# Moving three pieces of work inside the turns of a pipelined attention layer

## The chip, the cores and the metric

One core of a Trainium2 chip runs the whole program. The metric is the device time of one execution in microseconds (us). TensorE, VectorE, ScalarE, GpSimd and SyncE (the profile's PE, DVE, ACT, POOL and SP) each run an instruction list of their own, in order, and meet only at semaphores.

## The reference

Two layers over 16 sequences of 256 tokens with 256 features. Each layer adds to the running rows `x` the output of a sequence mixer and of a mixture of experts, both computed from the layer-normalised rows. The first layer's mixer is a state-space scan, the second's is causal attention with 16 heads of 16 features. Only that layer is touched:

```python
xn = _layernorm(x)                       # per token, over 256 features
qkv = (xn @ w_qkv).reshape(b, t, 3, 16, 16)
scores = einsum('bqhd,bkhd->bhqk', q, k) * 0.25      # causal mask, then softmax
out = einsum('bhqk,bkhd->bqhd', softmax(scores), v).reshape(b, t, d) @ w_o
gate = softmax(xn @ gate_w.T)            # top 2 of 8 experts per token
x = x + out + experts(xn)
```

## The kernel before

X holds all rows of `x` on chip. The program runs in four stages: the first layer's normalisation, routing and shared expert; its expert tiles; its scan; then the second layer's attention, and its expert tiles. The change lies in the attention.

**The attention as a pipeline.** `static(NSEQ, 5, attention, first=1)` unrolls turns t = 1 to 19. Turn t works on five sequences at once: c = t, a = t - 1, b = t - 2, d = t - 3, o = t - 4, each present only while it lies in 0 to 15. Roughly:

- c: `combine` adds the first layer's expert outputs to X, `norm_stats` and `norm_apply` normalise (the power of the variance is GpSimd's).
- a: transposes of the normalised rows, router logits, queries and keys; the top-2 choice of experts (`pick_experts`, once for two sequences, when a is odd), ranks and places of the tokens (`rank_sums`, `place_slots`, when a is even).
- b: scores of its four groups of heads, and their row maxima.
- d: transposed scores, exponentials (ScalarE), masks (GpSimd), weighted sums (`weigh`), transposes of the mixed rows (`turn_mixed`), division by the sums (`normalise`).
- o: transposes (`turn_out`), output projection (`project_out`), sum into X (`add_out`).

Each engine has a function `attention` whose statements are that engine's order within a turn, written by hand. No planner moves anything.

**TensorE's order in a turn** (L2071 on). `scores(h, s, t)` is called eight times. It computes plain scores for half h of the four heads of group `s`, whose maxima VectorE takes, and transposed scores for `t`, whose maxima are already folded into the queries. Between the calls stand `turn_maxima(d, 1)`, `values`, `weigh(d, 0)`, then `turn_out`, `values`, then `weigh(d, 1)`, `norm_stage`, then `project_out(o)`, then `turn_maxima(b, 0)`, the ranking, the logits, `weigh(d, 2)`, then queries and keys, and so on. The sixth call is `scores(1, now(2), now(0))`; for its second part it waits for `qp`, which `shift(b, 0)` gives. The second call waits in the same way for `shift(d, 1)`. Ahead of `turn_maxima(b, 0)` stands a wait for `add_out(o)`, since both use the same bank of PSUM; ahead of `turn_maxima(d, 1)` one for the copy of the second keys, for the same reason.

**VectorE's order** (L1546 on). `maxima(r, i, h)` (L1519) are four masked reductions for group i. `shift(r, j)` (L1527) subtracts the transposed maxima from the queries. `normalise` (L1536, L1538) waits for `turn_mixed`. `norm_stats` is L1067, L1071 and L1074, `add_out` L1544, `norm_apply` L1087, and `pick_experts(1, i, [1])`, the choice of the second expert, L1127 to L1137.

**ScalarE** copies queries (L997) and keys (L1003) out of PSUM with head masks, `mixed_copy` is L992, the exponentials are L979. All matmuls are recorded under L1677, a helper; transposes stand under their own lines (`turn_maxima` L2061, `turn_mixed` L2068).

Of the kernel before, what the change touches and what calls it, by code (L numbers as in the profile page):

```python
# [19 lines left out]
NSEQ, SEQ, D = 16, 256, 256  # L20
# [116 lines left out]
def of(n):  # L137

    return Round(n // 2, n % 2) if 0 <= n < NSEQ else None
# [42 lines left out]
def is_first(r):  # L182

    return isinstance(r.n, int) and r.n < 2
# [8 lines left out]
def program(nc, ctx, a, out):  # L193
# [864 lines left out]
    def _(eng):  # L1058
# [106 lines left out]
        def place_tokens(l, m):  # L1165
            rank_sums(l, m)
            place_slots(l, m)
# [339 lines left out]
        def stats_stage(r):  # L1507
            A["comb"].wait(eng, r.n)
            norm_stats(1, r)
# [12 lines left out]
        def shift(r, j):  # L1522

            A["m"].wait(eng, 2 * r.n + j)
            for e in range(2):
                q = QM[r.u][:, e, j, :]
                ins = stt(q, bank[5][:, 0:SEQ], head_mask[:, 1 - e:2 - e], q, ALU.mult, ALU.add)  # L1527
            A["qp"].mark(ins)
# [12 lines left out]
        def add_out(r):  # L1541
            A["wo"].wait(eng, r.n)
            xs = X[:, bass.ds(r.n * CH, CH), :].rearrange("p c d -> p (c d)")
            A["add"].mark(tt(xs, xs, bank[5], ALU.add))  # L1544

        def attention(c, a, b, d, o):  # L1546
            if b:
                maxima(b, 0, 0)
            if d:
                shift(d, 1)  # L1550
            if b:
                maxima(b, 0, 1)
            if c and c.n > 1:
                combine(c, [0])
            if b and not a:
                place_tokens(1, NSEQ // 2 - 1)
            if b:
                maxima(b, 1, 0)
            if c and c.n > 1:
                combine(c, [1])  # L1560
            if b:
                maxima(b, 1, 1)
            if b and not a:
                table_index(2)
            if c and c.n > 1:
                stats_stage(c)
            if o and not d:
                for i in range(FF[1]["ni"]):
                    gate_product(1, of(0), i)
                add_down(1, of(0))  # L1570
            if o:
                add_out(o)
            if a and a.n == SPLIT + 3:
                list_floats(1)
            if b:
                maxima(b, 2, 0)
                shift(b, 0)
            if a:
                if a.n:
                    logits_stage(1, a)  # L1580
                if a.v == 0 and not is_first(a):
                    rank_sums(1, a.i - 1)
                if a.n == SPLIT + 3:
                    list_done(1)
            if b:
                maxima(b, 2, 1)
            if a:
                if a.v == 0 and not is_first(a):
                    place_slots(1, a.i - 1)
                if a.n == SPLIT:  # L1590
                    table_index(1)
                    next_lists()
                if a.v == 1:
                    pick_experts(1, a.i, [0])
            if b:
                maxima(b, 3, 0)
            if c:
                norm_apply(1, c)
            if b:
                maxima(b, 3, 1)  # L1600
            if d:
                normalise(d)
            if a and a.v == 1:
                pick_experts(1, a.i, [1])
            if a and a.n == SPLIT + 1:
                table_tiles(1)
# [65 lines left out]
    def _(eng):  # L1672
# [328 lines left out]
        def keys(r, m):  # L2001
            if m:
                A["kc"].wait(eng, 2 * r.n)
            for k in range(KD):
                ins = mm(bank[5][:, m * SEQ:(m + 1) * SEQ], w_qkv[:, k, D + m * P:D + (m + 1) * P], xT[r.u][:, k, :], k == 0, k == KD - 1)
            A["k"].mark(ins)

        def scores(h, s, t):


            if s:
                r, i = s
                A["exp"][h].wait(eng, r.n * GROUPS + i, 3)
                if r.n == 0 and 0 < i < 3:
                    A["max"][h].wait(eng, i - 1)
                if h == 0 and i % 2 == 0:
                    A["qc"].wait(eng, 2 * r.n + i // 2)
                    A["kc"].wait(eng, 2 * r.n + i // 2)
            if t:
                r, i = t  # L2020
                n = r.n * GROUPS + i
                A["qp"].wait(eng, 2 * r.n + i // 2)
                if n + 2 < NSEQ * GROUPS:
                    A["max"][1 - h].wait(eng, n + 2)
                else:
                    A["exp"][1 - h].wait(eng, n - 1)
            for part in range(CH):
                if s:
                    r, i = s
                    c = part  # L2030
                    for q in (2 * h, 2 * h + 1):
                        band = slice(ROWS * q, ROWS * (q + 1))
                        last = mm(score[:, q, c * P:(2 * c + 1) * P], QM[r.u][band, i % 2, i // 2, c * P:(c + 1) * P],
                           KM[r.u][band, i % 2, i // 2, 0:(c + 1) * P], True, True)
                if t:
                    r, i = t
                    c = 1 - part
                    for q in (2 - 2 * h, 3 - 2 * h):
                        band = slice(ROWS * q, ROWS * (q + 1))
                        ins = mm(score[:, q, 2 * c * P:(2 + c) * P], KM[r.u][band, i % 2, i // 2, c * P:(c + 1) * P],  # L2040
                                 QM[r.u][band, i % 2, i // 2, c * P:SEQ], True, True)
            if t:
                A["t"][1 - h].mark(ins)
            if s:
                A["s"][h].mark(last)
# [25 lines left out]
        def attention(c, a, b, d, o):  # L2071
            now = lambda i: (b, i) if b else None
            held = lambda i: (d, i) if d else None
            if b and not b.n:
                M["add"].wait(eng, NSEQ - 1)
            scores(0, now(0), held(1))
            if d:
                if b:
                    A["kc"].wait(eng, 2 * b.n + 1)
                turn_maxima(d, 1)  # L2080
            if b and not a:
                A["qc"].wait(eng, 2 * b.n + 1)
                rank_tokens(1, NSEQ // 2 - 1)
            elif b:
                values(b, 0)
            if d:
                A["vc"].wait(eng, d.n)
                A["on"].wait(eng, d.n, 1)
                weigh(d, 0)
            scores(1, now(0), held(2))  # L2090
            if o and not d:
                eng.wait_ge(s_l1b, 16 * (3 + 2 * E + 1))
                ffn_up(1, of(0))
            if o:
                turn_out(o, d)
            if o and not d:
                ffn_down(1, of(0))
            if b and a:
                values(b, 1)
            scores(0, now(1), held(2))  # L2100
            if d:
                weigh(d, 1)
            if a:
                if b:
                    A["vc"].wait(eng, b.n)
                if a.n:
                    norm_stage(1, a)
            elif b:
                RT[1]["rkc"].wait(eng, NSEQ // 2 - 1)
                values(b, 0)  # L2110
                values(b, 1)
            scores(1, now(1), held(3))
            if o:
                project_out(o)
            scores(0, now(2), held(3))
            if b:
                if o:
                    A["add"].wait(eng, o.n)
                turn_maxima(b, 0)
            if a:  # L2120
                if a.v == 0 and not is_first(a):
                    N[1]["xT"].wait(eng, a.n)
                    rank_tokens(1, a.i - 1)
                if a.n == SPLIT + 3:
                    N[1]["xT"].wait(eng, a.n)
                    turn_list(1)
                if a.n:
                    logits_stage(1, a)
            if d:
                weigh(d, 2)  # L2130
            scores(1, now(2), now(0))
            if a:
                queries(a, 0)
                keys(a, 0)
            scores(0, now(3), now(0))
            if a:
                queries(a, 1)
            if d:
                weigh(d, 3)
            scores(1, now(3), now(1))  # L2140
            if d:
                turn_mixed(d)
            if a:
                keys(a, 1)
        eng.wait_ge(s_fill, 5)
        static(NSEQ, 5, attention, first=1)
        eng.wait_ge(s_slots, 2)
# [49 lines left out]
```

## Time and profile before

| what | value |
|---|---|
| time, three runs | 1500.08, 1507.12, 1514.33 us (median 1507.12) |
| profiled execution | 1499.64 us, its span 1497.9 us |
| busy, TensorE | 1368.1 us (91%) |
| busy, VectorE | 869.2 us (58%) |
| busy, GpSimd | 658.2 us (44%) |
| busy, ScalarE | 509.8 us (34%) |
| mean granted TensorE clock | 0.975 of full speed |
| chain that ended last | TensorE 79%, VectorE 11%, issue 5% |

Busy time is from the page's first part, over the whole span; the stages have different limits, so it says little about one of them. The rows below are from the attention. In a row of a timeline stand the start (us from the span's start), how long the merged group lasts, the engine, the line, the operation with its output and input, the number of instructions, and in brackets the engine's idle time before them with what ended it.

### The profile page before, as it was taken

To read this page: it belongs to the slowest core of one execution; us is meant where nothing else is said; L and a number is where in the kernel's file an instruction comes from. 1 tells how busy PE (TensorE), PEld (TensorE's weight loads), DVE (VectorE), ACT (ScalarE), POOL (GpSimd) and SP (SyncE) were. 2 spreads that over 40 slices of the span, in tenths; PEclk is the share of its full clock that TensorE was granted. 3 is DMA by queue.
4 is the path that set the end of the run, shared out by engine and by line. 5 is a ranking of instruction groups with operands and counts; after the bars stand their busy time and mean duration, and the time that the engine had idled before them with its cause. 6 is when DMAs were issued, how large, how long until landed. Compare 5 with 4: busy or idle time off the path is not lost.

```text
span 1497.9 us, 30015 instructions
## 1 busy us (share of the span) xinstructions
PE 1368.1 (91%) x10609; PEld 1120.7 (75%) x10625; DVE 869.2 (58%) x3075; ACT 509.8 (34%) x1102; POOL 658.2 (44%) x812
## 2 busy tenths in 40 slices
PE   7997999999999999899998899999988888878886
PEld 6886889999999999676665566666656566767775
DVE  4564434444444443689988788888877732322256
ACT  2221122222222222333343455555545342323331
POOL 2355423333333332555552244544534455666661
PEclk9998999999999999999999899999999998999998
DMA  5997811111111111500001011010100012222357
GB/s 183 141 118 66 105 52 50 47 47 50 51 49 46 49 50 37 173 1 0 0 0 43 23 44 44 23 44 24 44 23 16 2 33 81 78 82 84 111 186 234
DMA packets 69940, 94.90 MB, mean 63 GB/s; under 512 B 13401, under 2 KB 57433, under 8 KB 69808
## 3 DMA queue, kind: packets, MB, share of 16 engines
q1 hardware_dynamic: 51152, 53.92, 16.9%
q0 software_dynamic: 18656, 39.23, 8.5%
q8 instruction: 82, 1.34, 0.4%
q14 instruction: 50, 0.41, 0.1%
HBM read 60.66 MB, written 32.44 MB: 62 GB/s over the span
## 4 chain that ended last, share of the span: by engine, by line
PE 79%; DVE 11%; issue 5%; another core or an unknown queue 2%; ACT 1%; POOL 1%; DMA 0%; SPq 0%; DVEq 0%; POOLq 0%; ACTq 0%
PE score L1677 47%; PE mixed L1677 18%; PE side L1677 9%; DVE score L1519 4%; PE side L1897 2%; DVE WGU L1519 1%; DVE X L1500 1%; POOL ARENA L735 1%; PE side L2061 1%; DVE X L1634 1%; PE mixed L2068 1%; DVE stats L1067 1%; PE side L1687 1%; DVE X L1544 1%
## 5 line engine op out<-in xcount | busy, mean ns | idle before, releaser
L761 POOL DMA_INDIRECT XN<-xn_rows,slot_tok x111 | 109.5, 987 | 236.9 <-PE side L1897 205.7
L1677 PE MATMUL score<-xT,HT 128*128 128x128 f32 x1136 | 208.0, 275 | 0.0
L768 POOL DMA_INDIRECT y_rows<-sh_gu,slot_row x149 | 147.2, 988 | 131.9 <-ACT sh_gu L947 96.7
L1519 DVE CUSTOM_DVE_ANT_0 score<-score,future_b 128x128 f32<-128x128 f32 (+1 forms) x512 | 167.9, 390 | 64.1 <-PE score L1677 62.4
L796 POOL TENSOR_SCALAR_AFFINE_SELECT ARENA<-ARENA 128x256 f32<-128x256 f32 x256 | 103.5, 428 | 193.9 <-ACT ARENA L979 193.7
L1677 PEld LDWEIGHTS score<-xT,HT 128*128 128x128 f32 x1136 | 166.8, 192 | 0.0
L1294 DVE TENSOR_TENSOR HT<-sh_gu,score 128x128 f32<-128x128 f32 (+1 forms) x149 | 71.3, 478 | 150.8 <-ACT sh_gu L941 80.3
L979 ACT ACTIVATE ARENA<-score 128x768 f32<-128x768 f32 x128 | 104.2, 814 | 151.4 <-PE score L1677 151.2
L1677 PE MATMUL score<-ARENA 32*128 32x256 f32 (+1 forms) x2048 | 129.1, 358 | 24.4 <-DVE WGU L1519 13.7
L703 POOL DMA_INDIRECT lists<-token_no,w_in x128 | 125.4, 980 | 50.0 <-issue 26.2
L1269 DVE COPY xT<-WGU 128x256 f32 x142 | 45.9, 364 | 169.7 <-PE score L1677 168.9
L941 ACT ACTIVATE sh_gu<-score 128x128 f32<-128x128 f32 (+1 forms) x149 | 64.3, 432 | 210.5 <-PE score L1677 157.9
L1677 PE MATMUL mixed<-ARENA,HT 128*128 x568 | 134.4, 379 | 0.0
L947 ACT ACTIVATE sh_gu<-mixed 128x256 f32<-128x256 f32 x149 | 57.1, 384 | 224.2 <-PE mixed L1677 215.3
L735 POOL TENSOR_TENSOR ARENA<-tri_le,DT 128x1024 bf16<-128x1024 bf16 x48 | 90.2, 1894 | 87.4 <-PE mixed L1677 34.3
L1677 PEld LDWEIGHTS score<-ARENA 32*128 32x128 f32 x2048 | 75.6, 192 | 62.3 <-issue 44.4
L1677 PE MATMUL score<-XT,sh_gu 128*128 128x256 f32 x512 | 116.8, 388 | 1.2 <-DMA sh_gu<-in_sh_gu 1.2
L1677 PEld LDWEIGHTS mixed<-ARENA,HT 128*128 128x128 f32 x568 | 102.6, 190 | 11.0
L1677 PE MATMUL score<-xT 128*128 128x128 f32 x568 | 109.9, 275 | 1.0 <-ACT xT L935 1.0
L1677 PEld LDWEIGHTS score<-XT,sh_gu 128*128 128x128 f32 x512 | 98.9, 195 | 15.2 <-DMA sh_gu<-in_sh_gu 1.6
L1677 PE MATMUL score<-xT,sh_gu 128*128 128x128 f32 x568 | 109.8, 275 | 0.0
L1677 PE MATMUL score<-xT,WGU 128*128 128x128 f32 x624 | 84.1, 278 | 7.1 <-ACT xT L935 5.8
(248 smaller groups left out, 2674.7 us busy)
## 6 DMA issues: line engine op xcount, KB each, us to landing
WGU<-in_gu SPq DMA_DIRECT2D x8, 1024.0 KB
WGU<-y_rows SPq DMA_DIRECT2D x32, 256.0 KB, 3.2
ARENA<-y_rows SPq DMA_DIRECT2D x32, 256.0 KB
xn_rows<-XN SPq DMA_DIRECT2D x24, 256.0 KB
X<-in_u SPq DMA_DIRECT2D x16, 256.0 KB
ARENA<-in_dn SPq DMA_DIRECT2D x8, 512.0 KB
out<-X SPq DMA_DIRECT2D x16, 256.0 KB
y_rows<-sh_gu,slot_row POOLq DMA_INDIRECT x149
```

The source lines that it names most:

```text
L703: eng.indirect_dma_start(lists[l], bass.IndirectOffsetOnAxis(slot_l[:, k, t:t + 1], 0), tok_i[:, k, t:t + 1], None).then_inc(s_scat[g], 16)
L735: ins = eng.tensor_tensor(MHm[:, a, :, :, :].rearrange("p c h t -> p (c h) t"), tri_le[:, :].unsqueeze(1).broadcast_to([P, CH * MH, P]), a ...
L761: x["got"][j % ring].mark(eng.indirect_dma_start(XG[j % ring], None, xn_rows[l], bass.IndirectOffsetOnAxis(slot_tok[:, j:j + 1], 0)))
L768: x["out"][j % RING].mark(eng.indirect_dma_start(y_rows[g], bass.IndirectOffsetOnAxis(slot_row[:, j:j + 1], 0), YO[j % RING], None))
L796: ins = eng.affine_select(out=m, in_=m, compare_op=ALU.is_ge, fill=0.0, base=0, pattern=[[0, 2], [1, P]], channel_multiplier=-1)
L941: x["sg"].mark(act(SE[:, 0:w], bank[r.u][:, 0:w], ACT.Silu))
L947: x["yo"].mark(act(YO[r.v], bank[6 + r.u][:, 0:D], ACT.Copy))
L979: A["exp"][h].mark(act(PT[i % 2][:, 2 * h:2 * h + 2, :, :].rearrange("p r b q -> p r (b q)"), score[:, 2 * h:2 * h + 2, 0:HALVES * P], ACT ...
L1269: ins = eng.tensor_copy(to, wgu0[:, bass.ds(expert(r), 1), k, first * P:end * P].rearrange("p a (c n) -> p (a c) n", n=P))
L1294: x["h"].mark(tt(HET[r.u][:, 0:w // P, :], parts(SE[:, 0:w]), parts(up), ALU.mult))
L1519: ins = eng.tensor_tensor_reduce(s, s, future, -1.0, BIG, ALU.add, ALU.min, NM[:, c, j, at:at + 1])
L1677: return eng.matmul(o, l, r, start=start, stop=stop)
```

## The change

Three moves, two on VectorE and one on TensorE; no instruction is added or removed.

- VectorE: `stats_stage(c)` moves from ahead of `add_out(o)` to behind it.
- VectorE: `pick_experts(1, ., [1])`, the choice of the second expert, moves from the end of the turn in which a is odd to the next turn, where that sequence is b, between `shift(d, 1)` and `maxima(b, 0, 1)`. For the last sequence it stays at the end.
- TensorE: at the end of the turn, `keys(a, 1)` moves ahead of `turn_mixed(d)`.

```diff
@@ VectorE, attention @@
             if d:
                 shift(d, 1)
+            if a and b and b.v == 1:
+                pick_experts(1, b.i, [1])
             if b:
                 maxima(b, 0, 1)
...
             if b and not a:
                 table_index(2)
-            if c and c.n > 1:
-                stats_stage(c)
             if o and not d:
                 for i in range(FF[1]["ni"]):
                     gate_product(1, of(0), i)
                 add_down(1, of(0))
             if o:
                 add_out(o)
+            if c and c.n > 1:
+                stats_stage(c)
             if a and a.n == SPLIT + 3:
                 list_floats(1)
...
             if d:
                 normalise(d)
-            if a and a.v == 1:
+            if a and a.n == NSEQ - 1:
                 pick_experts(1, a.i, [1])
@@ TensorE, attention @@
             scores(1, now(3), now(1))
+            if a:
+                keys(a, 1)
             if d:
                 turn_mixed(d)
-            if a:
-                keys(a, 1)
```

## Rows read from the trace of the kernel before

**Rows 1.** A stretch: its length, PE, PEld, DVE, ACT, POOL busy, PEclk, DMA, GB/s.

```profile
864.42:1150.43 286.01, 264.30 (x3061) 178.36 (x3060) 238.72 (x1159) 155.16 (x264) 133.96 (x253) 0.99 0.11 33
```

**Rows 2.** Waits of TensorE, 864 to 1150 us: total, times, longest.

```profile
PE side L2061 <- DVE X L1544: 5.6, 12, 0.5
PE side L2061 <- ACT ARENA L1003: 2.7, 11, 0.2
```

**Rows 3.** Timeline of TensorE, the turn of an even b.

```profile
1003.70 0.94 PE L1677 MATMUL score<-ARENA 32*128 32x128 f32 x16
...
1006.90 0.94 PE L1677 MATMUL score<-ARENA 32*128 32x128 f32 x16
...
1014.81 0.94 PE L1677 MATMUL score<-ARENA 32*128 32x128 f32 x16
1016.21 0.44 PE L2061 MATMUL side<-ident,WGU 128*128 128x128 f32 x2 [0.47 <-DVE X L1544]
...
1017.37 0.86 PE L1677 MATMUL mixed<-ARENA,WGU 128*32 128x256 f32 x16
1018.27 0.94 PE L1677 MATMUL score<-ARENA 32*128 32x128 f32 x16
...
1024.64 1.09 PE L2068 MATMUL mixed<-ident,sh_gu 128*128 128x128 f32 x8
1025.57 1.03 PE L1677 MATMUL side<-xT,WGU 128*128 128x256 f32 x4
1026.53 0.94 PE L1677 MATMUL score<-ARENA 32*128 32x128 f32 x16
```

**Rows 4.** Timeline of VectorE and GpSimd in the same turn, round the output sum.

```profile
1014.21 0.75 DVE L1067 BATCH_NORM_STATS2 stats<-X 128x6 f32<-128x256 f32 x2
...
1015.48 0.68 DVE L1544 TENSOR_TENSOR X<-X,side 128x512 f32<-128x512 f32 x1
...
1016.08 0.28 DVE L1519 CUSTOM_DVE_ANT_0 score<-score,future_b 128x128 f32<-128x128 f32 x1
...
1017.30 0.86 DVE L1527 SCALAR_TENSOR_TENSOR ARENA<-side,head_mask,ARENA 128x256 f32<-128x256 f32 x2
...
1017.55 0.72 POOL L694 TENSOR_TENSOR rstd<-rstd,minus_half 128x2 f32<-128x2 f32 x1
```

**Rows 5.** Timeline of TensorE, the next turn (odd b).

```profile
1030.49 0.94 PE L1677 MATMUL score<-ARENA 32*128 32x128 f32 x16 [0.69 <-DVE ARENA L1527]
...
1038.24 0.94 PE L1677 MATMUL score<-ARENA 32*128 32x128 f32 x16
...
1041.84 0.94 PE L1677 MATMUL score<-ARENA 32*128 32x128 f32 x16
...
1044.63 0.94 PE L1677 MATMUL score<-ARENA 32*128 32x128 f32 x16
```

**Rows 6.** Timeline of both engines in turn 16, which has no statistics.

```profile
1161.61 0.94 PE L1677 MATMUL score<-ARENA 32*128 32x128 f32 x16
...
1161.72 0.69 DVE L1544 TENSOR_TENSOR X<-X,side 128x512 f32<-128x512 f32 x1 [0.57 <-issue]
```

**Rows 7.** Timeline of VectorE round the start of an odd turn.

```profile
1026.09 0.35 DVE L1536 RECIPROCAL WGU<-mixed 128x32 f32<-128x32 f32 x1
...
1027.08 0.18 DVE L1127 TENSOR_REDUCE route_small<-w_in 128x4 f32<-128x32 f32 x1
...
1028.30 0.29 DVE L1519 CUSTOM_DVE_ANT_0 score<-score,future_b 128x128 f32<-128x128 f32 x1
...
1031.45 0.30 DVE L1519 CUSTOM_DVE_ANT_0 score<-score,future_b 128x128 f32<-128x128 f32 x1 [1.06 <-PE score L1677]
```

**Rows 8.** Timeline of TensorE at three long waits or behind them.

```profile
849.98 1.63 PE L1677 MATMUL score<-ARENA 32*128 32x128 f32 x16 [1.54 <-DVE WGU L1519]
...
858.92 0.94 PE L1677 MATMUL score<-ARENA 32*128 32x128 f32 x16
...
1130.81 0.94 PE L1677 MATMUL score<-ARENA 32*128 32x128 f32 x16 [2.27 <-DVE ARENA L1527]
```

## What the change is expected to do

> **What bounds the kernel now.** I read the page's slices first, then busy time by stretch, TensorE's waits, and the rows of each engine in order of time. The change touches only the second layer's attention, about 817 to 1215 us of the span. Its middle is twelve turns, 286.01 us (one of them is stretched by `table_index`), with TensorE busy for 264.30 us and VectorE for 238.72 us [rows 1]. Both are nearly full, so each step must be asked which of the two comes last.
>
> A turn has eight calls of `scores`; I call them S1 to S8 and measure between their starts. In the turn of an even sequence b, S1 is at 1003.70, S2 at 1006.90, S5 at 1014.81, S6 at 1018.27 and the next S1 at 1026.53: 22.83 us [rows 3]. The odd turn behind it has S2 at 1030.49, S5 at 1038.24, S6 at 1041.84 and S7 at 1044.63 [rows 5]. Three waits of TensorE matter: `turn_maxima(b, 0)` on `add_out` (X L1544, 12 times, about 0.47 us each), `turn_maxima(d, 1)` on the copy of the second keys (L1003, 11 times, 0.24 us each) [rows 2], and in odd turns S2 on `shift(d, 1)` (L1527, 0.69 us) [rows 5]. The change moves what stands ahead of all three. The rows show what comes last once they are gone.
>
> **Output sum ahead of the statistics.** Before, VectorE starts `norm_stats` at 1014.21, and what follows runs without a gap: statistics 1.27 us (to 1015.48), sum 0.60 (to 1016.08), four maxima 1.22 (to 1017.30), `shift(b, 0)` 0.86 (to 1018.16), and S6 begins at 1018.27 [rows 3, 4], 2.19 behind the sum's end. S6 needs `shift(b, 0)`, its `qp` wait. So this is one chain of 4.06 us that ends where S6 starts. TensorE comes there at about the same time: `weigh(d, 2)` starts at 1017.37 and lasts 0.86 [rows 3]. In the odd turn TensorE has the ranking too, 0.15 us, and S6 is at S5 + 3.60, in the even one at S5 + 3.46.
>
> The pieces are the same after, but the sum now comes first, and it cannot start when VectorE is free (1014.21, S5 - 0.60): it waits for `project_out`, which ends as S5 begins. The one turn that has a sum and no statistics shows when that is: S5 at 1161.61, the sum at 1161.72 after 0.57 us idle [rows 6], S5 + 0.11. Then 0.60 + 1.27 + 2.19 = 4.06, and S6 comes at S5 + 4.17 in turns of both kinds. The wait of `turn_maxima` goes: before, it starts 0.73 after the sum does (1016.21 against 1015.48), so the sum now frees it at S5 + 0.84 and TensorE comes at S5 + 0.87. But TensorE is then ready for S6 at about S5 + 2.85 (1018.2, the end of `weigh`, less the 0.5 us that it no longer waits, counted from 1014.81), and waits there for some 1.3 us instead. Statistics and sum stand together in the turns with c and o, t = 4 to 15: six even ones at +0.71 (4.17 - 3.46), six odd ones at +0.57 (4.17 - 3.60), **+7.7 us**. If the wake-up is 0 or 0.18 us instead of 0.11, it is 6.4 or 8.5. GpSimd's power of the variance, which waits for the statistics, starts at 1017.55 [rows 4], behind a mask; the statistics would now be ready at 1014.81 + 0.11 + 0.60 + 1.27 = 1016.79, so that this delay stays hidden, and with it `norm_apply`, SP's store behind it and the loads queued behind that store. If that cover went, the factor would still have until `norm_apply`, which stands eight maxima further on.
>
> **Second keys ahead of the transposes.** Nothing is added. TensorE gives 0.93 us to `turn_mixed` and 0.96 to the keys (1024.64, 1025.57, 1026.53 [rows 3]), and they change places. The keys' copies on ScalarE start 0.93 us earlier and the 0.24 us before `turn_maxima(d, 1)` go. But `normalise(d)` on VectorE reads these transposes. Before, they ended at 1025.73 and the reciprocal came without waiting at 1026.09 [rows 7], S1 - 0.44, S1 being that of the next turn. After, they run from S1 - 0.93 to S1 + 0.16, and the reciprocal comes at S1 + 0.27 to 0.34 (I take 0.30). The division ends 0.99 later (1027.08 [rows 7]), the four maxima take 1.22 and the shift, up to the start behind it, 0.97 (1017.30 to 1018.27 [rows 3, 4]): S2 = S1 + 3.50. Even turns had 3.20 (1003.70 to 1006.90), where VectorE idled before the first maxima and TensorE was not held at S2. So they lose 0.30, seven times: +2.1. The gain on TensorE is behind this, and is lost.
>
> **Second expert choice behind the shift.** Six small operations, from 1027.08 to 1028.30, 1.22 us, which stood ahead of the odd turn's first maxima [rows 7]. They move behind `shift(d, 1)`, where VectorE idles for 1.06 us before its next maxima at 1031.45 [rows 7]: they fit but for some 0.08 us, given the wait for S2. Odd turns go from 3.96 to 3.50 at S2 and give back 0.08: six turns, -2.3. The first odd turn (b = 1) has no transposes and no wait of this kind, and I take it as zero. The last (b = 15) keeps the choice at its old place and gets the later reciprocal as well: about +0.85. What the later S2 does to the step behind it I take as nothing; 0.15 us in seven turns either way is 1 us. The two moves together: 2.1 - 2.3 + 0.85, **+0.7 us**, between -1.5 and +2.
>
> **Sum.** +8.4 us, bounds +5 and +10.5. The profiled execution took 1499.64 us (span 1497.9 and 1.7 around it), the three runs 1500.08 to 1514.33, median 1507.12. On the profiled execution the sum gives 1508.0, on the median 1515.5; the four times have a mean of 1505.3, and from it come 1513.7, rounded to **1514 us**. About 1% (15 us) is what a measurement of this kernel can tell from no change, so I forecast a small loss that reads as the same.
>
> **Rival A, slower: the new wait drops TensorE's clock.** The waits of 1.3 us at S6 would be the longest of each turn. At 849.98 TensorE had waited 1.54 us and its next 16 matmuls took 1.63 us instead of 0.94; S5 to S7 took 8.94 us (to 858.92 [rows 8]) against 6.39 in a usual odd turn (1038.24 to 1044.63 [rows 5]): 2.55 us for one fall from 2.4 to 1.2 GHz. Against it: at 1130.81 a wait of 2.27 us left the duration at 0.94 [rows 8], and 0.69 us did no harm in any odd turn. 1.3 is between, but nearer the one that did. It decides from three falls in twelve turns (8.4 + 7.65 = 16.1 us, over 1%); six give 23.7, so 1529. Chance 0.20. The Trainium skill (TensorE: Matmul & The Clock Gate, HAM oscillation) describes kernels in which a wait that recurs in every iteration takes the clock down each time. By it the price would be paid twelve times, 1505.3 + 8.4 + 30.6 = 1544; the row at 1130.81 speaks against every time.
>
> **Rival B, faster: the waits go and nothing takes their place.** 5.6 us at the output sum and 2.7 at the keys' copy [rows 2], and 0.76 us in six odd turns (3.96 less 3.20), 4.6: -12.9, so 1492. It needs S6 to be free of VectorE's order, and the rows show 0.11 us between the shift's end and S6 [rows 3, 4]. Chance 0.07.
>
> **Rival C: no change.** VectorE idles 47 of 286 us in the twelve turns [rows 1], 3.9 a turn; if the statistics' delay were taken up there, the time would stay 1505. But that idle time lies behind S2 and S6 and moves with them. Chance 0.13.
>
> **How the numbers follow.** Forecast 0.60, A 0.20, C 0.13, B 0.07. The range runs from 1500 (C with a low run) to 1529 (A with six falls). Faster by over 1%: only B's far end, 0.03. Slower by over 1%: A, and 0.03 of the forecast, 0.23. Within 1%: 0.74.
>
> **What would show it.** In the same turns after: the sum at S5 + 0.11 behind 0.7 us of idle VectorE; S6 at S5 + 4.17 behind a wait of 1.1 to 1.35 us on the shift (L1527); no wait on X L1544; S1 to S2 3.50 in turns of both kinds; the reciprocal waiting for the transposes (L2068); both kinds of turn some 23.8 us long (even: 22.83 + 0.71 + 0.30). The forecast is wrong if S5 to S6 stays under 3.7, if the clock of the stretch, 0.99 before [rows 1], falls under 0.95, or if anything outside the attention moves by more than 3 us.

## The result and the profile after

| | before | after |
|---|---|---|
| median (lowest to highest), us | 1510.54 (1500.08 to 1519.54), 10 runs | 1521.03 (1516.18 to 1526.38), 10 runs |
| ratio to before, 95% interval | | 1.0088 (1.0059 to 1.0117) |
| profiled execution, us | 1499.64, span 1497.9 | 1524.96, span 1523.2 |

The change makes the kernel 0.9% slower by the ratio, whose interval does not reach 1; between the medians it is 10.5 us, 0.7%. One execution of the kernel before, among those of the first set of experiments, took 2712.81 us and is left out of the ratios. From here on "after" is the changed kernel. Two lines more stand ahead of TensorE's helpers in it, so L1677 of before is L1679, L2061 is L2063 and L2068 is L2070; VectorE's lines are the same.

The first three views answer to [rows 1 to 5]. First the stretch of twelve turns, S1 of turn 4 to S1 of turn 16, with the columns of [rows 1], then TensorE's waits in it (total us, times, longest).

```profile
867.75:1160.62 292.87, 266.16 (x3062) 181.40 (x3061) 241.02 (x1158) 155.29 (x265) 133.47 (x253) 0.98 0.11 32
...
PE score L1679 <- DVE ARENA L1527: 15.8, 13, 1.9
PE score L1679 <- DVE WGU L1519: 6.5, 21, 3.1
PE score L1679 <- issue: 3.7, 11, 0.3
```

The stretch went from 286.01 to 292.87 us. Both waits that the change aimed at, on X L1544 and on the copy of the keys [rows 2], are gone. In their place stands one on the shift, L1527, 13 times: twelve at S6 and one at S2 of turn 15, the 1.9.

TensorE in turn 10 (b even) and in turn 11 (b odd), in order of time: S1, S2, S5, the transposes, the third `weigh`, S6, S7; then S2, S5 and S6 of turn 11.

```profile
1009.38 0.94 PE L1679 MATMUL score<-ARENA 32*128 32x128 f32 x16
...
1012.68 0.94 PE L1679 MATMUL score<-ARENA 32*128 32x128 f32 x16 [0.34 <-issue]
...
1020.48 0.94 PE L1679 MATMUL score<-ARENA 32*128 32x128 f32 x16
1021.35 0.44 PE L2063 MATMUL side<-ident,WGU 128*128 128x128 f32 x2
...
1022.51 0.86 PE L1679 MATMUL mixed<-ARENA,WGU 128*32 128x256 f32 x16
...
1024.65 1.67 PE L1679 MATMUL score<-ARENA 32*128 32x128 f32 x16 [1.28 <-DVE ARENA L1527]
...
1029.03 0.94 PE L1679 MATMUL score<-ARENA 32*128 32x128 f32 x16
...
1037.85 0.94 PE L1679 MATMUL score<-ARENA 32*128 32x128 f32 x16 [0.34 <-issue]
...
1045.70 0.94 PE L1679 MATMUL score<-ARENA 32*128 32x128 f32 x16
...
1049.87 0.94 PE L1679 MATMUL score<-ARENA 32*128 32x128 f32 x16 [1.04 <-DVE ARENA L1527]
```

The transposes no longer wait: they start at S5 + 0.87 rather than at S5 + 1.40. TensorE is done 0.5 us sooner and then stands 1.28 us before S6, which begins at S5 + 4.17 (1024.65 less 1020.48); before it was S5 + 3.46 [rows 3]. In the odd turn it is again S5 + 4.17, behind a wait of 1.04. S1 to S2 is 3.30 in both. The even turn shown is one of the two turns in which the clock fell behind the wait: the 16 matmuls at 1024.65 took 1.67 us, the granted clock from there to 1028.00 was 0.50, and S7 came 4.38 us later instead of 2.79.

VectorE in the same turn: the reciprocal at its start, then the sum, the statistics, the first of four maxima, the shift.

```profile
1009.49 0.36 DVE L1536 RECIPROCAL WGU<-mixed 128x32 f32<-128x32 f32 x1 [0.46 <-PE mixed L2070]
...
1020.59 0.69 DVE L1544 TENSOR_TENSOR X<-X,side 128x512 f32<-128x512 f32 x1 [0.57 <-PE side L1679]
1021.19 0.75 DVE L1067 BATCH_NORM_STATS2 stats<-X 128x6 f32<-128x256 f32 x2
...
1022.45 0.29 DVE L1519 CUSTOM_DVE_ANT_0 score<-score,future_b 128x128 f32<-128x128 f32 x1
...
1023.67 0.87 DVE L1527 SCALAR_TENSOR_TENSOR ARENA<-side,head_mask,ARENA 128x256 f32<-128x256 f32 x2
```

VectorE idles 0.57 us for the projection's end, where it used to run the statistics [rows 4]. The rest of the chain has its old length and so ends that much later. The idle time, and the 0.11 between S5 and the sum, are just what turn 16 had shown before [rows 6].

The steps of a turn in us, read from the starts of S1 to S8 (the last step leads to the next S1; most turns agree within 0.02):

```
                 S1-2 S2-3 S3-4 S4-5 S5-6 S6-7 S7-8 S8-1   turn
before, even     3.20 2.65 2.48 2.79 3.46 2.79 2.72 2.76  22.84
before, odd      3.96 2.48 2.48 2.79 3.59 2.79 2.73 2.76  23.58
after, even      3.30 2.54 2.48 2.79 4.17 2.79 2.72 2.80  23.59
after, odd       3.30 2.58 2.48 2.79 4.17 2.79 2.72 2.80  23.62
```

Turn by turn the even ones cost 0.74 more (four times; 0.57 in turn 14), the odd ones 0.04 (four times). Turn 10 has a clock fall on top (+2.34 in all), turn 15 another (+1.63). Turn 13, stretched by `table_index` to a wait of 3.15 us ahead of S8, came out 0.85 shorter, since fewer of its matmuls ran at the lower clock (the 16 of S8 took 1.00 us instead of 1.67). Together 6.8 us.

**Where the other 19 us of the two profiled executions are.** They differ by 25.3 us. The code ahead of turn 2 is the same, and took 5.4 us more (to S1 at 822.8 against 817.4). The attention from S1 of turn 2 to S1 of turn 18 took 389.5 against 383.1 us, 6.4 more. The unchanged remainder, nearly all of it the last expert stage, took 310.9 against 297.4, 13.5 more. On the three chips of the timed experiments and the last pair that remainder took 248 to 249 us in all kernels alike. So the single pair of profiles overstates the change, and only its attention part is read below. That part holds some luck too. Ahead of S5 of turn 3 TensorE waits 1.54 us in both kernels. Behind it the clock fell in before [rows 8] and not in this profile of after:

```profile
856.27 0.94 PE L1679 MATMUL score<-ARENA 32*128 32x128 f32 x16 [1.54 <-DVE WGU L1519]
...
859.44 0.94 PE L1679 MATMUL score<-ARENA 32*128 32x128 f32 x16
```

That turn took 25.04 us before and 22.14 after, so 2.9 us of the price of the change are missing from the 6.4 by this alone. In `after_again` below, the same kernel, it fell, and the turn took 25.14.

### The profile page after: what moved, and what is told of

It reads as the page before. It is cut to its first block, busy times and chain, and to the rows that moved or that the text cites. A ratio compares the mean times of both kernels' runs of the same rounds, so it can differ in the third digit from the quotient of the medians.

```text
span 1523.2 us, 30015 instructions
## 1 busy us (share of the span) xinstructions
PE 1376.9 (90%) x10609; PEld 1128.7 (74%) x10625; DVE 870.7 (57%) x3075; ACT 511.3 (34%) x1102; POOL 655.4 (43%) x812
## 4 chain that ended last, share of the span: by engine, by line
PE 76%; DVE 12%; issue 4%; another core or an unknown queue 4%; DMA 2%; ACT 1%; SPq 0%; DVEq 0%; POOL 0%; ACTq 0%; POOLq 0%
PE score L1679 45%; PE mixed L1679 16%; PE side L1679 9%; DVE score L1519 4%; PE side L1899 2%; DMA xn_rows<-ARENA 2%; DVE WGU L1519 1%; DVE ARENA L1527 1%; PE mixed L2070 1%; DVE stats L1067 1%; DVE ARENA L1413 1%; DVE X L1636 1%; DVE X L1500 1%; PE side L1833 0%
## 5 line engine op out<-in xcount | busy, mean ns | idle before, releaser
L1679 PE MATMUL score<-xT,HT 128*128 128x128 f32 x1136 | 208.0, 275 | 0.0
L796 POOL TENSOR_SCALAR_AFFINE_SELECT ARENA<-ARENA 128x256 f32<-128x256 f32 x256 | 103.1, 426 | 201.0 <-ACT ARENA L979 200.7
L1679 PEld LDWEIGHTS score<-xT,HT 128*128 128x128 f32 x1136 | 166.8, 192 | 0.0
L1679 PE MATMUL score<-ARENA 32*128 32x256 f32 (+1 forms) x2048 | 128.0, 355 | 38.6 <-DVE ARENA L1527 19.2
L1679 PE MATMUL mixed<-ARENA,HT 128*128 x568 | 134.4, 379 | 0.0
L1679 PEld LDWEIGHTS score<-ARENA 32*128 32x128 f32 x2048 | 74.9, 189 | 74.1 <-issue 58.5
L1679 PE MATMUL score<-XT,sh_gu 128*128 128x256 f32 x512 | 117.5, 389 | 11.6 <-remote 10.4
L1679 PEld LDWEIGHTS score<-XT,sh_gu 128*128 128x128 f32 x512 | 98.9, 195 | 26.0 <-remote 10.8
L1679 PE MATMUL score<-xT 128*128 128x128 f32 x568 | 109.9, 275 | 1.0 <-ACT xT L935 1.0
L1679 PEld LDWEIGHTS mixed<-ARENA,HT 128*128 128x128 f32 x568 | 102.6, 190 | 11.0
L1679 PE MATMUL score<-xT,sh_gu 128*128 128x128 f32 x568 | 109.8, 275 | 0.0
L1239 DVE TENSOR_TENSOR HT<-SG,score 128x256 f32<-128x256 f32 x96 | 39.7, 419 | 99.3 <-ACT SG L852 76.4
```

Of the source, the lines that this page charges most:

```text
L796: ins = eng.affine_select(out=m, in_=m, compare_op=ALU.is_ge, fill=0.0, base=0, pattern=[[0, 2], [1, P]], channel_multiplier=-1)
L1679: return eng.matmul(o, l, r, start=start, stop=stop)
```

## The experiments

Two sets of timed kernels ran on two further chips, both some 50 us faster than the first: the kernel before took 1456.41 us there (first set) and 1457.12 (second). Three kernels were executed singly at the end.

**The sum ahead of the statistics, alone (first set).**

```diff
-            if c and c.n > 1:
-                stats_stage(c)
...
             if o:
                 add_out(o)
+            if c and c.n > 1:
+                stats_stage(c)
```

> Only the output sum is moved ahead of the statistics; keys and second expert choice stay where they were. Chain theory (the statistics now stand between the late sum and shift(b, 0)): S5 to S6 4.17 us in all twelve turns with c and o, S1 to S2 as before (3.20 in even turns, 3.96 in odd ones), so +0.71 and +0.57 a turn, +7.7 us against the kernel before, some more for falls of the clock. Theory that the later transposes of turn_mixed make the loss: no slower than before, and S5 to S6 about 3.0. Theory that the clock makes it: S5 to S6 4.17 too, but most of the loss is in slow matmuls behind S6, at least three falls in the twelve turns.

Measured: 1466.22 us, ratio 1.0061 (1.0031 to 1.0092). TensorE, S5 and S6 of an even turn:

```profile
1025.03 0.94 PE L1677 MATMUL score<-ARENA 32*128 32x128 f32 x16
...
1029.20 0.94 PE L1677 MATMUL score<-ARENA 32*128 32x128 f32 x16 [1.28 <-DVE ARENA L1527]
```

S5 to S6 is 4.17, in all twelve turns, with every other step of a turn as in `before_pair` below (even 23.40, odd 24.14). There is no clock fall behind any S6, though the waits are the same 1.28 and 1.04 us. This one move carries most of the loss, +0.6% of 0.7 to 0.9, and without a fall behind S6.

**The two other moves, without that one (first set).** The keys ahead of `turn_mixed`, the second choice behind `shift(d, 1)`, and the sum left where it was.

```diff
 @@ VectorE @@
+            if a and b and b.v == 1:
+                pick_experts(1, b.i, [1])
             if b:
                 maxima(b, 0, 1)
...
-            if a and a.v == 1:
+            if a and a.n == NSEQ - 1:
                 pick_experts(1, a.i, [1])
 @@ TensorE @@
+            if a:
+                keys(a, 1)
             if d:
                 turn_mixed(d)
-            if a:
-                keys(a, 1)
```

> Only the second expert choice and the second keys are moved; the output sum stays behind the statistics. Chain theory: S5 to S6 3.46 and 3.60 as before; S1 to S2 3.30 in both kinds of turn (what the changed kernel shows) against 3.20 and 3.96; turns of about 22.9 and 23.0 us against 22.83 and 23.58, so about -3 us. Theory that the later transposes make the loss: slower than before by 5 us or more.

Measured: 1459.39 us, ratio 1.0017 (0.9991 to 1.0042). Even turns 22.95, odd 23.14; S5 to S6 is without the delay, 3.59 and 3.72. The twelve turns took 282.99 us, against 285.23 in `before_pair`; what was gained there was given back in turn 17, 30.26 us, where S1 to S2 is 4.60 and a clock fall stretches S3 to S4 to 5.24. The expected -3 us held for the clean turns and not for the whole: the time cannot be told from before, nor from the prediction's +0.7 for these two moves.

**The wait at S6 filled with matmuls (first set).** After, and the third `weigh` issues its matmuls twice in turns with both a and o, with the same result.

```diff
-        def weigh(r, i):
+        def weigh(r, i, twice=False):
...
+            for again in range(2 if twice else 1):
                 for t in range(CH):
                     for hd, row in heads(i):
...
             if d:
-                weigh(d, 2)
+                weigh(d, 2, twice=a is not None and o is not None)
             scores(1, now(2), now(0))
```

> The changed kernel with the 16 matmuls of weigh(d, 2) issued twice in the turns with a and o (0.79 us more TensorE work in each, same result), in front of S6, where TensorE waits 1.04 to 1.28 us. Chain theory: S5 to S6 stays 4.17, the wait shrinks to 0.25 to 0.5 us, and only the falls of the clock behind it go: two in the profiled execution at about 1.6 us each, so 2 to 4 us faster than the changed kernel. Clock theory: all of the loss comes back, 10 us faster than the changed kernel. If TensorE and not VectorE set S6, the doubled work would cost 0.79 us in 12 turns, 9.5 us slower than the changed kernel.

Measured: 1467.07 us, ratio 1.0059 (1.0025 to 1.0092). The twelve turns and two waits of them (columns as above):

```profile
876.62:1166.73 290.11, 271.90 (x3254) 185.81 (x3253) 238.26 (x1158) 156.90 (x265) 133.60 (x253) 0.99 0.11 33
...
PE score L1679 <- DVE WGU L1519: 5.8, 17, 3.1
PE score L1679 <- DVE ARENA L1527: 5.7, 7, 1.9
```

192 more matmuls (3254 against 3062) and S6 still at S5 + 4.16, behind waits of 0.63 us in even turns and 0.39 in odd ones: TensorE's work there is free, VectorE's chain alone sets the step. No clock fall follows S6 in any turn, and the twelve turns are 2.1 us shorter than in the profile of the next kernel. The times do not show the expected gain of 2 to 4 us over the changed kernel: its ratio beside the second set, 1.0069, is not apart from 1.0059.

**After once more, beside the second set.**

> The changed kernel once more, beside the single parts. Chain theory: as in its first profile, S1 to S2 3.30 and S5 to S6 4.17 in all twelve turns, +8 to +10 us against the kernel before, with a fall of the clock behind S6 in none to two of them, since the output sum alone had none and lost 0.61%. Clock theory: three or more falls behind S6, and a loss that grows with their number.

Measured: 1465.91 us, ratio 1.0069 (1.0041 to 1.0096). The same steps on another chip (even 23.51, odd 23.57), and again two clock falls behind S6, in the same turns 10 and 15 (S6 to S7 4.27 and 4.43). The attention from S1 of turn 2 to S1 of turn 18 took 389.7 us.

**The statistics later still (first set).** After, but with the statistics behind `shift(b, 0)` and just ahead of the next group's maxima.

```diff
             if o:
                 add_out(o)
-            if c and c.n > 1:
-                stats_stage(c)
...
                     list_done(1)
+            if c and c.n > 1:
+                stats_stage(c)
             if b:
                 maxima(b, 2, 1)
```

> The changed kernel with the statistics moved further back on VectorE, behind shift(b, 0), the logits and the rank sums, just ahead of maxima(b, 2, 1). Chain theory: S6 is then free of them and comes at S5 + 2.9 in even and 3.0 in odd turns, where TensorE itself is ready; the statistics (1.27 us) delay the maxima behind S6 by 0.3 to 0.5 us, hidden in even turns and costing some 0.3 at S8 in odd ones. Turns of about 22.3 and 22.8 us, so about -8 us against the kernel before and -18 against the changed one. Clock or transposes theory: no faster than the kernel before.

Measured: 1456.16 us, ratio 0.9994 (0.9969 to 1.0018). The wait on the shift at S6 is gone (0.29 us is left in even turns) and S5 to S6 is 3.17, but not the 2.9 that the chain without the statistics would give. The sum ended 0.79 behind S5, and the maxima then waited 0.17 us for S5's own scores. Odd turns pay 0.23 and 0.26 at the next two steps, where the statistics now stand ahead of maxima that TensorE wants. Even turns are 22.53 and odd ones 23.08, the twelve turns 282.74 us against 290 to 293 with the sum directly ahead of the statistics; turn 17 took 30.25 us and gave back some 3. It is 10 us faster than `sum_only` in the same set, where 18 over the changed kernel was expected, and the expected gain of 8 over before did not come; that the 1.27 us of statistics inside the chain are what costs stands.

**The second choice moved, alone (second set).**

```diff
+            if a and b and b.v == 1:
+                pick_experts(1, b.i, [1])
             if b:
                 maxima(b, 0, 1)
...
-            if a and a.v == 1:
+            if a and a.n == NSEQ - 1:
                 pick_experts(1, a.i, [1])
```

> Only the second expert choice is moved, behind shift(d, 1) of the next turn. The reciprocal does not wait for the transposes, so odd turns should have S1 to S2 at 3.20 like the even ones, instead of 3.96, and give back 0.06 at S3: -0.7 us in each of six turns, and nothing else changes: about -4 us against the kernel before (-0.3%). If the moved choice delays maxima(b, 0, 1) for good, S2 to S3 grows by the same 0.7 and the time stays.

Measured: 1453.66 us, ratio 0.9968 (0.9942 to 0.9993). TensorE, S1, S2 and S3 of an odd turn:

```profile
1028.75 0.94 PE L1679 MATMUL score<-ARENA 32*128 32x128 f32 x16
...
1031.95 0.94 PE L1679 MATMUL score<-ARENA 32*128 32x128 f32 x16
...
1034.45 0.94 PE L1679 MATMUL score<-ARENA 32*128 32x128 f32 x16
```

S1 to S2 falls from 3.96 to 3.20 (the wait of 0.69 in [rows 5] is gone) and S2 to S3 rises by 0.03 only. This move is a gain by itself, 0.72 us in each odd turn (22.97 against 23.69 in `before_pair`).

**The keys moved, alone (second set).**

```diff
+            if a:
+                keys(a, 1)
             if d:
                 turn_mixed(d)
-            if a:
-                keys(a, 1)
```

> Only the second keys go ahead of turn_mixed. If the transposes' lateness costs what the changed kernel shows, even turns have S1 to S2 3.30 instead of 3.20 and odd ones about 4.55 (reciprocal at S1 + 0.11, division 0.99, the choice 1.22, maxima 1.22, shift 0.97: 4.51), against 3.96; with S8 to S1 0.04 longer, +0.1 and +0.6 a turn, +4 us in twelve turns and some 0.7 more in turn 17. If the move did what it looks like, the 0.24 us in front of turn_maxima(d, 1) would be gained in each turn, -3 us.

Measured: 1466.50 us, ratio 1.0055 (1.0017 to 1.0093). VectorE at the start of an odd turn, then TensorE's S1 and S2 of that turn:

```profile
1038.84 0.36 DVE L1536 RECIPROCAL WGU<-mixed 128x32 f32<-128x32 f32 x1 [0.46 <-PE mixed L2068]
1039.23 0.69 DVE L1538 TENSOR_TENSOR ARENA<-mixed,WGU 128x512 f32<-128x512 f32 x1
1039.84 0.17 DVE L1127 TENSOR_REDUCE route_small<-w_in 128x4 f32<-128x32 f32 x1
...
1041.15 0.28 DVE L1519 CUSTOM_DVE_ANT_0 score<-score,future_b 128x128 f32<-128x128 f32 x1
...
1038.73 0.94 PE L1677 MATMUL score<-ARENA 32*128 32x128 f32 x16
...
1043.34 0.94 PE L1677 MATMUL score<-ARENA 32*128 32x128 f32 x16 [1.65 <-DVE ARENA L1527]
```

The reciprocal waits for the transposes, and the whole choice of experts (1.3 us) now stands behind it: S1 to S2 is 4.61 in odd turns, a wait of 1.65 us. So at this step the move costs 0.65 in each odd turn alone, but only 0.10 once the choice is out of its way (3.20 against 3.30). The step shows that the moves depend on each other: keys and choice add up to a gain of 0.11 in an odd turn (+0.65, -0.76), and together they gain 0.66. The whole times do not show it. The single ratios, +0.61%, -0.32% and +0.55%, make +0.84% against +0.69% and +0.88% measured for all three, and the last two make +0.23% against +0.17% for the pair, with intervals of some 0.3% on each side.

**The mix that should win (second set).** Sum ahead, statistics late, the choice moved, the keys left at their old place.

> The output sum first, the statistics late (just ahead of maxima(b, 2, 1)), the second expert choice moved, and the keys left behind turn_mixed. Put together from what the single parts showed: even turns S1 to S2 3.20, S5 to S6 3.17, 22.4 us; odd turns 3.20, 3.17 and some 0.5 lost at S7 and S8, 22.9 us; against 22.83 and 23.58 before that is -0.4 and -0.7, -6.5 us in twelve turns, and turn 17 keeps its 27.1 to 27.4 us. About -7 us against the kernel before (-0.45%).

Measured: 1447.58 us, ratio 0.9934 (0.9902 to 0.9967), faster than both kernels. TensorE's waits in its twelve turns (277.91 us):

```profile
PE score L1679 <- DVE WGU L1519: 7.4, 24, 3.5
PE side L2063 <- ACT ARENA L1003: 2.9, 12, 0.2
PE score L1679 <- issue: 1.7, 6, 0.3
PE score L1679 <- DVE ARENA L1527: 1.0, 1, 1.0
```

Neither X L1544 nor, but for turn 15, the shift holds TensorE. Even turns take 22.40, odd 22.91. The wait for the keys' copy, 0.24 us each, which the keys' move would take away, is back and is the cheaper of the two.

**Why the step before was 3.46 on one chip and 3.59 on others.** Both sets showed S5 to S6 at 3.59 and 3.72 wherever the statistics still came first, 0.13 more than [rows 3, 5]. The kernel before again, twice, and the choice's move beside the second:

> The kernel before once more, on the chip of the experiments, to read S5 to S6. In pick_only, keys_only and no_sum, none of which touches these steps, it is 3.59 in even and 3.73 in odd turns, while the first profile of the kernel before has 3.46 and 3.60; the difference is one small instruction of the statistics (L1074) at 0.31 us instead of 0.17. If the two moved parts cause it, this run has 3.46 and 3.60 again; if it depends on the run or the chip, it has 3.59 and 3.73, and the output sum's price there is 0.57 and 0.44 a turn instead of 0.71 and 0.57.

Measured: 1510.01 us, on a chip as slow as the first: 3.46 and 3.58.

> The kernel before and pick_only on one chip, since before_again ran on another chip than pick_only did and so does not tell chip from kernel. If the chip sets the duration of L1074, it is the same here in both kernels (0.17 or 0.31 us in both), and S5 to S6 is 3.46 and 3.60 or 3.59 and 3.73 in both.

> See before_pair. If the kernel sets it, L1074 takes 0.17 us in before_pair and 0.31 here, S5 to S6 is 3.59 and 3.73 here, and moving the choice gives back 0.76 us at S2 in odd turns but loses 0.13 at S6 in every turn.

Measured on one chip: 1443.05 and 1433.86 us, each from one execution (another of the kernel before on that chip took 1449.88, so the two times say little). S5 to S6 is 3.59 and 3.72 in both, so it does not come from an edit. The last operation of the statistics differs (shortest, median, longest in ns); first the kernel before as first profiled, then `before_pair`:

```profile
L1074 DVE TENSOR_SCALAR rstd<-mv x10: 169/170/184, 876.1 to 1085.3; 128x2 f32<-128x2 f32 x10
```

```profile
L1074 DVE TENSOR_SCALAR rstd<-mv x11: 311/314/320, 870.1 to 1105.9; 128x2 f32<-128x2 f32 x11
```

With the statistics first it took 0.17 us on the first chip and that of `before_again`, and 0.31 on the three chips of the other experiments. With the sum first (six profiles, on the first chip and two of those three) it took 0.17 each time. So neither chip nor order alone decides. Ahead of it one row differs: GpSimd's mask (L796) started 0.31 behind S5 on the first chip and 0.09 behind it in `before_pair`, with VectorE's own statistics at the same place. But the mask runs over L1074 in both. That its earlier start lengthens L1074 was not tried, and the cause stays open. For the change it means that the sum's move costs 0.71 and 0.57 us a turn (7.7 us) against before on the first chip, and 0.57 and 0.44 (6.1 us) on those three.

## Why the prediction was right, step by step

**The output sum.** The forecast took one chain, from the sum to S6, and let it begin at S5 + 0.11 because turn 16 did [rows 6]. It came out so: 0.57 us idle, S6 at S5 + 4.17, in twelve turns of twelve, in the four profiles of `after`, `after_again`, `sum_only` and `fill`, on three chips. The expected wait of TensorE was "some 1.3 us"; it was 1.28 and 1.04. `fill` shows by an addition that TensorE's side of the join does not count, `stats_late` by a removal that the statistics in the chain do. The term of +7.7 us is right on the first chip.

**The keys.** The mechanism was as forecast: the reciprocal waits for the transposes and the gain on TensorE is lost behind it. Its size was not. The reciprocal came at S1 + 0.11, not + 0.30. The transposes started at S1 - 0.97 (1008.41, 1.04 us long) and so ended at S1 + 0.07, where I had + 0.16, and the wake-up behind them was 0.04, where I had allowed 0.11 to 0.18. (The pieces named in the prediction also add up to 3.48, not to its 3.50.) So S2 is S1 + 3.30 instead of + 3.50: even turns lose 0.10 rather than 0.30, odd turns gain 0.66 rather than 0.46. Against that the step from S8 to the next S1 grew by 0.04 in every turn, which nothing in the sum foresaw, and S2 to S3 by 0.08 to 0.11 in odd turns, where 0.08 was expected. Even turns instead shortened there, from 2.65 to 2.54, which on the chips of the timed experiments (2.49 to 2.48) does not appear. For the two moves together the twelve turns of the pair (282.99 us against 285.23) say -2.2, where the forecast's terms give -0.5 (six by +0.30, six by -0.38); turn 17 (b = 15) said more than +0.85. S1 to S2 rose by 0.75 there, as forecast, and a clock fall mostly came with it: S3 to S4 is 5.15 to 5.74 in five of the six profiles with the keys first (3.58 in `after_again`), 5.02 in `best`, and 3.58 in the three of the kernel before, in `sum_only` and in the two with the choice alone. Turn 17 took 29.5 us on average in the six and 26.9 in the seven others, 2.7 more. The rows in after:

```profile
1186.28 0.17 PE L1679 MATMUL side<-hot_b,before_b 128*128 128x8 bf16 x1 [1.33 <-DVE hot_b L1137]
...
1188.24 1.51 PE L1679 MATMUL score<-ARENA 32*128 32x128 f32 x16 [0.87 <-DVE ARENA L1527]
```

Two waits, 1.33 and 0.87 us, that end 1.96 us apart, and then matmuls at the lower clock. Before, the first of them was 0.27 us.

**The choice.** Forecast as fitting into 1.06 us of idle VectorE but for 0.08. Alone it cost 0.03 at S2 to S3 and brought 0.76 at S2.

**Rival A, the clock.** It exists, but is not the cause. In both profiles of after the clock fell behind two of the twelve waits at S6, from 2.4 to 1.2 GHz for the 16 matmuls behind it; each fall cost 1.5 to 1.6 us (4.27 to 4.43 against 2.79), less than the 2.55 of [rows 8]. (The fall of [rows 8] itself cost 3.0: without it S5 to S7 of turn 3 took 5.96 in after, not the 6.39 of a later turn.) The two falls make 3.2 of the 6.9 us of the twelve turns in the first profile. It is not the cause of the loss: `sum_only` has the same waits and no fall behind them, `fill` has none either, and both are slower than before by 0.6%. The prediction also held against A that a wait of 2.27 us had left the clock up [rows 8]. It did so in `before_again` too, but not everywhere. In `before_pair`, the same kernel, the clock fell at the next step:

```profile
1122.71 0.94 PE L1677 MATMUL score<-ARENA 32*128 32x128 f32 x16 [2.26 <-DVE ARENA L1527]
...
1125.75 1.67 PE L1677 MATMUL score<-ARENA 32*128 32x128 f32 x16
```

In `sum_only` it fell there as well. That row was thin evidence for a small A. The Trainium skill (TensorE: Matmul & The Clock Gate, HAM oscillation) tells of a matmul kernel that loses the clock in every iteration behind a wait for DMA. In that example of the Trainium skill the wait is some 3 to 5 us, more than twice the waits at S6, so reading it as a price paid twelve times went further than that section. Ten of the twelve turns did not pay, and `sum_only` paid behind none of its twelve waits at S6.

**Rival B, a pure gain,** needed S6 to be free of VectorE's order. It was not. What B describes exists, but needs the statistics out of the chain and the keys left alone: `best`.

**Rival C, no change,** put the delay into VectorE's idle time. There is such time (51.9 of 292.87 us in the stretch), but it lies behind the joins, as the forecast said.

**The sum.** The forecast was +8.4 us on the clean steps, 7.2 of it in the twelve turns (six by 0.71 + 0.30, six by 0.57 - 0.38). Clean turns show six by 0.74 and six by 0.04, 4.7 us: the difference is the keys' term. The two falls bring 3.2 more and turns 13 and 14 take 1.1 off again, which makes the 6.8 measured. The medians show +10.5 us on the first chip (1.0059 to 1.0117: 9 to 18 us) and +8.8 on the chip of the second set (6 to 14). The attention from turn 2 to turn 18 is 6.4 us longer in the first pair of profiles, with turn 3 in its favour, and 8.9 longer from `before_pair` to `after_again` (389.7 against 380.8), two chips.

The granted clock of the whole execution, on record for each timed run, says more of the clock's part than single profiles can. In the second set it is 0.9826 on average in 35 executions of before and 0.9788 in 12 of after; in the first, 0.9825 and, in 12 of `sum_only`, 0.9808. The five kernels with the keys first on those chips lie at 0.9785 to 0.9796, the other three at 0.9808 to 0.9838. An estimate from these: 0.0038 of 1465 us is 5.6 us for the changed kernel if TensorE set the pace wherever the clock was low, so at most that, and 2.5 us for `sum_only`. Most of this goes with the keys' move: `no_sum`, which has no waits at S6, is at 0.9789. So the total fits partly by luck, because misses cancel: the keys' term was 2.4 us too dear in the twelve turns and some 1.8 too cheap in turn 17, and the falls of the clock were in no term. How the clock's part divides over the turns stays open, since most kernels have one profile.

**A criterion that did not hold.** I had written that the forecast is wrong if anything outside the attention moves by over 3 us. The stretch ahead of turn 2 moved by 5.4 and the tail by 13.5 in the first pair of profiles, with no change in their code, so by that sign the forecast would have been wrong. On the other three chips the tail lay between 248.0 and 249.1 us, but S1 of turn 2 came anywhere from 806.0 to 829.2. That limit should have been put on times of several runs.

## What to carry to other kernels

A wait that an engine's order removes comes back wherever the next join of the same two engines lies, so follow both engines' chains to that join before counting the wait as a gain: here 0.5 us went at the first join and 0.7 was lost at the next. Moving a piece that must wait ahead of a piece that need not puts the second into the chain; the piece without a deadline (the statistics) belongs behind the last operation that the other engine waits for. Moves that look alike in kind are to be timed apart and together: of three, one paid, two cost, and the cost of one depended on another being there.

## What the runs showed of the hardware

- Waits of one length do not decide the clock. Twelve waits of 1.28 or 1.04 us at one place: two falls in after (the same two turns in two profiles on different chips), none in `sum_only`; in `fill`, where doubled matmuls left 0.63 and 0.39 of them, none either. The same wait of 1.54 us ahead of S5 of turn 3 was followed by a fall in ten of the thirteen profiles and not in `after`, `stats_late` and `best`. One of 2.27 us left the clock up in `before` and `before_again`; in `before_pair` and `sum_only` it fell one step later. One of 3.15 us ahead of S8 of turn 13 left it up in `before_pair`.
- A fall behind S6 cost 1.5 to 1.6 us, the one in turn 3 3.0, not the 2.55 that the prediction used.
- Chips differ by more than the change: the last expert stage and what follows took 297 and 311 us on the first chip, 300 on that of `before_again` and 248 to 249 on three others, with the same code; whole runs 1510 against 1456 us.
- One small operation (128x2, L1074) took 0.17 or 0.31 us, depending on chip and on the order of the work around it, steadily within a run; what sets it was not found.
